# Moving weight splits and time-mix rows to other blocks of a fused FFN stage, and re-ordering the time-mix lists

## The reference, cut to what matters

```python
x = x + 0.5 * L0_ffn(layernorm(x))      # 8 experts, top 2, softmax; shared width 2 x 128
x = x + L0_attn(layernorm(x))           # RWKV: time mix (scan over 256 steps), then channel mix
x = x + 0.5 * L0_ffn(layernorm(x))
x = x + 0.5 * L1_ffn(layernorm(x))      # 8 experts, top 2, sigmoid; shared width 4 x 128
x = x + L1_attn(layernorm(x))           # Mamba-2 with chunks
x = x + 0.5 * L1_ffn(layernorm(x))
```

```python
kvr = norm1(x) @ W_tm;  k, v, r = split(kvr, 3)
k = k * tmk + x_prev * (1 - tmk)        # likewise v; r goes through a sigmoid
y = wkv(time_decay, time_first, k, v)   # recurrence with a running log-sum-exp
x = x + r * y
xn = norm2(x); kk = xn @ W_cm * cmk4 + xp4 * (1 - cmk4)
x = x + sigmoid(xn * cmr + xp * (1 - cmr)) * (square(relu(kk)) @ W_cp)
```

## Time and profile before

| what | value |
|---|---|
| median of 3 runs | 798.79 us (797.66 to 799.57) |
| profiled execution | 803.27 us, of which the span from first to last instruction is 801.5 us |
| mean granted TensorE clock | 0.931 |
| busy share of the span | PE 87%, DVE 71%, ACT 52%, POOL 40% |
| first FFN stage, until PE's first instruction of the next | 142.25 us |
| RWKV stage | 142.25 to 240.3 us |
| all stages behind it | 240.3 to 801.5 us |

### The profile page before, as it was taken

One profiled execution on the slowest core, in us unless ns is written; L12 is line 12 of the kernel. 1 busy time (PEld: TensorE's weight loads), 2 busy tenths in 40 slices (PEclk: granted clock), 3 DMA queues, 4 the chain that ended last, 5 costly groups with the idle time before them and its releaser, 6 DMA issues. The chain is left out here.

```text
span 801.5 us, 12341 instructions
## 1 busy us (share of the span) xinstructions
PE 693.8 (87%) x3996; PEld 511.4 (64%) x3996; DVE 571.6 (71%) x1283; ACT 417.0 (52%) x751; POOL 322.3 (40%) x402
## 2 busy tenths in 40 slices
PE   0979995649887899999999767899999995899997
PEld 0657773324344677777778556677777773677785
DVE  3668796588976888889878675456556665698775
ACT  2535564866523555555555547355555552555553
POOL 1346697210112676545635541322222200356355
PEclk9989997759998999999999967699999997899999
DMA  5244550000000422312122100000000000132222
GB/s 151 87 119 120 151 164 13 0 1 0 2 0 20 140 84 77 105 66 94 59 86 72 49 0 1 1 2 2 1 0 0 0 1 1 68 91 83 77 91 69
DMA packets 32757, 43.10 MB, mean 54 GB/s; under 512 B 5184, under 2 KB 15424, under 8 KB 32704
## 3 DMA queue, kind: packets, MB, share of 16 engines
q1 hardware_dynamic: 32704, 42.46, 17.3%
HBM read 41.13 MB, written 1.31 MB: 53 GB/s over the span
## 5 line engine op out<-in xcount | busy, mean ns | idle before, releaser
L526 POOL TENSOR_TENSOR p_prod<-p_p,p_gate_row 128x512 f32<-128x512 f32 x128 | 201.5, 1583 | 149.6 <-DVE p_p L397 94.5
L303 ACT ACTIVATE p_sil<-p_ps_a 128x512 f32<-128x512 f32 x176 | 105.3, 598 | 142.0 <-PE p_ps_a L100 137.9
L402 DVE TENSOR_TENSOR p_hlo<-p_prod,p_hhi 128x512 fp32r<-128x512 f32 x176 | 152.5, 868 | 0.9 <-ACT p_hhi L312 0.5
L397 DVE TENSOR_TENSOR p_p<-p_sil,p_ps_b 128x512 f32<-128x512 f32 x128 | 87.2, 681 | 64.0 <-ACT p_sil L303 51.1
L312 ACT CAST p_hhi<-p_prod 128x512 fp32r<-128x512 f32 x176 | 108.1, 614 | 31.7 <-POOL p_prod L526 31.4
L98 PE MATMUL p_ps_acc<-p_hhi,w_downhi 128*128 128x512 f32 x176 | 73.0, 415 | 5.2 <-DVE p_hlo L402 5.1
L98 PE MATMUL p_ps_a<-xt_hi,w_uphi 128*128 128x512 f32 x176 | 75.2, 427 | 0.0
L98 PE MATMUL p_ps_b<-xt_hi,w_uphi 128*128 128x512 f32 x176 | 71.7, 407 | 1.6 <-DVE p_p L397 1.2
L99 PE MATMUL p_ps_a<-xt_lo,w_uphi 128*128 128x512 f32 x176 | 70.9, 403 | 0.0
L100 PE MATMUL p_ps_a<-xt_hi,w_uplo 128*128 128x512 f32 x176 | 70.9, 403 | 0.0
L100 PE MATMUL p_ps_b<-xt_hi,w_uplo 128*128 128x512 f32 x176 | 70.6, 401 | 0.0
(11 more groups left out here) (277 smaller groups left out, 1445.2 us busy)
## 6 DMA issues: line engine op xcount, KB each, us to landing
p_gate_row<-gate_rows SPq DMA_DIRECT2D x128, 256.0 KB, 3.3
w_rawbuf<-in_L_ffn_fc_w_dram SPq DMA_DIRECT2D x3, 512.0 KB, 6.3
w_rawbuf<-in_L_ffn_w_dram SPq DMA_DIRECT2D x3, 512.0 KB, 6.0
out_dram<-x SPq DMA_DIRECT2D x4, 256.0 KB, 3.7
w_rawbuf<-in_L_ffn_shared_w_dram SPq DMA_DIRECT2D x3, 256.0 KB, 5.1
mb_xraw<-in_L_attn_W_B_dram SPq DMA_DIRECT2D x1, 512.0 KB, 4.9
mb_xraw<-in_L_attn_W_C_dram SPq DMA_DIRECT2D x1, 512.0 KB, 5.1
gate_rows<-p_gates_t SPq DMA_DIRECT2D x16, 16.0 KB, 1.4
```

The lines of the kernel that those rows point to most:

```text
L303: nc.scalar.activation(sil[:, u % 2], ps_a[:, u % 2], ACT.Silu).then_inc(c["sil"].sem, 1)
L397: nc.vector.tensor_tensor(dst, sil[:, u % 2], ps_b[:, u % 2], ALU.mult).then_inc(c["p1"].sem, 1)
L402: nc.vector.tensor_tensor(hlo[:, u % R], prod[:, u % R], hhi[:, u % R].bitcast(F32), ALU.subtract).then_inc(c["hlo"].sem, 1)
L526: G.tensor_tensor(prod[:, u % R], p1[:, u % 2], gate_row[:, e % ROWS], ALU.mult).then_inc(c["prod"].sem, 1)
```

## The change

The loads change places, the splits go to other slots, three blocks' rows are made in the FFN stage, and the RWKV lists are in another order. `ytok` and `ztok` have four buffers each; `z2tok` and `rg` lose theirs and use the block's `ytok` and `ztok`. The router becomes part 2 of the six weight parts, for both FFNs' weights.

```diff
-    SPLIT_SLOTS = {(2, 5): 0, (2, 6): 1, (2, 7): 2, (3, 0): 3, (3, 3): 4, (3, 5): 5}
+    POOL_SPLITS = {(1, 6): (0,), (1, 7): (1,), (1, 8): (2,), (2, 6): (3,)}
+    DVE_SPLITS = {(BLOCKS - 1, 8): (4, 5)}
+    SPLITS = {**POOL_SPLITS, **DVE_SPLITS}
+    TAIL = BLOCKS - 1
+    NEXT_STATS = {(TAIL - 1, 4): 0, (TAIL - 1, 8): 1, (TAIL, 8): 2}
+    NEXT_SCALES = {(TAIL - 1, 7): 0, (TAIL, 2): 1, (TAIL, 8): 2}
+    NEXT_ROWS = {(TAIL, 1): (0, 0), (TAIL, 2): (0, 1), (TAIL, 5): (1, 0), (TAIL, 6): (1, 1)}
...
@@ ffn_stream, ACT
-                    if splits and (n, p) in SPLIT_SLOTS:
-                        split_hi(nc, act, c, splits[SPLIT_SLOTS[n, p]])
-                    if entry and (n, p) == (BLOCKS - 1, U - 2):
-                        next_tokens(0)
+                    for k in SPLITS.get((n, p), ()) if splits else ():
+                        split_hi(nc, act, c, splits[k])
+                    if entry and (n, p) in NEXT_ROWS:
+                        next_rows(*NEXT_ROWS[n, p])
                 take_out(n)
...
             if entry:
-                next_tokens(1)
+                next_rows(2, 0)
+                next_rows(2, 1)
@@ ffn_stream, DVE: next_stage(n, p), behind gated, low, add_out, choose, normal, low_x, measure
+                if (n, p) in NEXT_STATS:
+                    next_stats(NEXT_STATS[n, p])
+                if (n, p) == (TAIL, 3):
                     prepare_vectors(nc, dve, c, entry["vec"])
+                if (n, p) == (TAIL, 5):
                     prepare_mixing(nc, dve, c, entry["vec"], consts, entry, entry["weights"])
+                    for k in DVE_SPLITS.get((n, p), ()) if splits else ():
+                        split_lo(nc, dve, c, splits[k], k)
...
@@ rwkv_phase, PE
             mix_key(0)
+            mix_key(1)
             mix_val(0)
-            mix_key(1)
...
@@ rwkv_phase, ACT (first entries)
+            take_z(0)
             take_y(0)
-            take_z(0)
+            take_z(1)
             take_y(1)
-            take_z(1)
-            tokens(2)
+            tokens(3)
             decays(0)
-            tokens(3)
             logs(0)
             decays(1)
...
@@ rwkv_phase, DVE
-            measure(2)
             measure(3)
             running_max(0)
...
@@ program
-            jobs.append(((EXPERTS,), [(lambda r: r, router)]) + tuple(t[:] for t in w.router))
+            jobs.insert(2, ((EXPERTS,), [(lambda r: r, router)]) + tuple(t[:] for t in w.router))
...
         def load_rest(sp):
-            w1_set.load(sp, slice(3, None))
-            mb.load(sp)
+            w1_set.load(sp, slice(4, None))
+            rw_set.load(sp)
...
-                           loads=(rw_set.load, lambda sp: w1_set.load(sp, slice(0, 3)), load_rest) if k == 0 else (),
+                           loads=(lambda sp: w1_set.load(sp, slice(0, 4)), load_rest, mb.load) if k == 0 else (),
```

More of the change, by code:

```diff
@@ L565, in body @@
                         scale(n + 3)
[L566 to L569, removed]
+                    for k in POOL_SPLITS.get((n, p), ()) if splits else ():
+                        split_rest(k)
+                    if entry and (n, p) in NEXT_SCALES:
+                        scale_norms(nc, pool, c, consts, entry, NEXT_SCALES[n, p])
             scale(0)
@@ L660, in scale_norms, with apply_norm @@
     G.tensor_tensor(r[:, 5:7], r[:, 2:4], r[:, 4:5].broadcast_to([P, 2, BT]), ALU.mult).then_inc(c["r_rs"].sem, 1)
[L663 to L668, removed]
+def apply_norm(nc, x, entry, m, which):
+    dst, scale, bias = (("ytok", 2, 5), ("ztok", 3, 6))[which]
+    for j in range(BT):
+        r = entry["rs"][:, m]
+        last = nc.scalar.activation(entry[dst][m][:, j], x[:, m * BT + j], ACT.Identity, bias=r[:, bias, j:j + 1],
+                                    scale=r[:, scale, j:j + 1])
     return last
@@ L833, in _ @@
             mix_key(2)
+            grow(2)
             turn_z2(1)
             shrink(0)
+            grow(3)
+            turn_in(3)
             mix_val(2)
-            turn_in(3)
-            grow(2)
+            mix_key(3)
             shrink(1)
-            grow(3)
+            shrink(2)
             mix_rec(2)
-            mix_key(3)
-            shrink(2)
             shrink(3)
@@ L859, in _ @@
             grow(8)
+            grow(9)
             turn_x2(3)
-            grow(9)
+            grow(10)
             shrink(8)
-            grow(10)
             grow(11)
@@ L935, in receive @@
                     act.wait_ge(c["r_p"].sem, c["r_p"].at(m - 1))
-                A(rg[h][:], mixed[4][:], ACT.Tanh, scale=0.5).then_inc(c["r_tr"].sem, 1)
+                A(gate_of(m), mixed[4][:], ACT.Tanh, scale=0.5).then_inc(c["r_tr"].sem, 1)
             def shifted_k(m):
@@ L957, in tokens2 @@
                 for j in range(BT):
-                    last = A(z2tok[h][:, j], key_bank(m)[:, bass.ts(j, P)], ACT.Identity, bias=rs[h][:, 3, j:j + 1],
+                    last = A(ytok[m][:, j], key_bank(m)[:, bass.ts(j, P)], ACT.Identity, bias=rs[h][:, 3, j:j + 1],
                              scale=rs[h][:, 1, j:j + 1])
@@ L1190, in _ @@
             apart(0)
-            lead2(1)
             blend(0)
             output(0)
+            lead2(1)
             received(0)
+            residual(0)
             parts2(1)
-            residual(0)
-            wrap(0)
+            measure2(0)
             numerator(1)
-            measure2(0)
             numerators(1)
@@ L1214, in _ @@
             parts(2)
+            shift(2)
+            square(2)
+            total(2)
+            shift(3)
             gate_in(1)
-            total(2)
-            square(1)
-            shift(2)
             lead2(2)
-            square(2)
+            running_max(3)
             parts2(2)
-            shift(3)
             square(3)
+            lead(3)
             numerator(2)
+            parts(3)
             numerators(2)
-            running_max(3)
-            lead(3)
             gated(0)
-            parts(3)
             apart(2)
+            total(3)
+            blend(2)
             shift(4)
-            blend(2)
-            total(3)
             output(2)
@@ L1255, in _ @@
             received(3)
-            gate_in(2)
             residual(3)
@@ L1263, in _ @@
             square(9)
-            wrap(3)
             shift(10)
+            gate_in(2)
             square(10)
@@ L1268, in _ @@
             square(11)
+            wrap(3)
             gated(2)
-            gate_in(3)
             shift(12)
             square(12)
+            gate_in(3)
             add_out(2)
@@ L2022, in program @@
         for n in ("ytok", "ztok"):
-            entry[n] = [owned(rwkv_scope)(f"rw_{n}{h}", [P, BT, P], F32) for h in range(2)]
+            entry[n] = [owned(rwkv_scope)(f"rw_{n}{h}", [P, BT, P], F32) for h in range(NBLK)]
         entry.update(vec=v, weights=rw)
```

76 lines of the change are left out of this document (39 added, 37 removed).

## The result

The changed kernel takes 788.41 us (median of 4 runs, 786.25 to 791.30), the kernel before 799.18 beside it; the ratio is 0.986, with a 95% interval from 0.982 to 0.991, so 10.8 us less, where 15.8 were forecast. The profiled execution took 788.62 us with a span of 786.9, 14.6 us less than the span of before. That is more than the medians show, since the profiled execution of before (803.27 us) was 4.1 us above the median of the runs beside it. Terms of one or two us are therefore read from the stages in the traces, and the medians only checked against their sum.

A forecast was written before the change was run, and what follows sets the result against it. PE bounds the kernel, busy 87% of the span, losing time where it runs dry or its clock is down; VectorE bounds the later RWKV stage. 5.9 + 0 + 5.4 + 4.5 = 15.8 us, giving 783.0 us; range 777 to 791.

The forecast's parts named there:

- the 18 DMAs: RWKV loads, moved behind row 7 of block 1: block 2's first product 2.3 us late, cost 0, at most 3 us.
- the forecast itself: Outcome of the whole run with a gain of 11 to 18 us, given a chance of 0.57.
- rival 1: Half the gain, 8 us: row 4 late, clock falls, VectorE waits as before; or splits hold VectorE; chance together 0.22.
- The early loads: First FFN's start: row 4 lands 3.1 us earlier, clock stays up for 2.8 more; 5.9 us, bounds 1.4 and 7.1.
- the text's own sign of being wrong: Row 4 still waits for bytes, PE idles in block 1 or 2, or VectorE's idle from the first shift grows.
- the early hole: First FFN: PE dry for 4.85 us since GpSimd waits for row 4 of block 0, with block 1's gates behind.
- The late hole: First FFN's end: earlier last product, sum's copy ahead of row making; 5.4 us, bounds 3.5 and 7.5.
- The RWKV stage: New list order: logs(0) 3.1 us sooner, first shift 3.4, net 1.1 more; 4.5 us, bounds 1.5 and 6.5.
- Rival 2: Whole run: all three parts near their upper bounds, 19.6 us less, 779 us; chance 0.15.
- rival 3: Slower than before: the 18 DMAs delay block 2's rows, first landing at 104 or later; 800 or more, chance 0.04.

The follow-up runs named there:

- e1: Changed kernel with the RWKV stage's three engine lists in the old order (third block's rows stay in the FFN stage); ratio 0.9933 to the kernel before.
- e3: Changed kernel with the 18 RWKV DMAs issued at the FFN stage's start, before the store of block 0's gates; ratio 0.985 to the kernel before.
- e10: Changed kernel with the fourth block's rows, tokens(3), again between decays(0) and logs(0) in ScalarE's RWKV list; ratio 0.990 to the kernel before.
- e2: Changed kernel with VectorE's two splits of the last block moved behind the last add_out; ratio 0.986 to the kernel before.
- e5: Changed kernel measured again without any edit, as the yardstick; 790.00 us, ratio 0.9885 to the kernel before.
- e6: Changed kernel with VectorE's two splits behind the last add_out and GpSimd's fourth split behind its last scales; ratio 0.987 to the kernel before.
- e7: Kernel before with only the load places of the changed one; ratio 0.9967 to the kernel before.
- e4: Changed kernel with weight parts 0 to 3 issued at the FFN stage's start, not between rows 3 and 4 of block 0; ratio 0.983 to the kernel before.
- e8: Changed kernel with weight and RWKV loads at the stage's start, late splits last, third block's statistics and scales earlier, mixing diagonals later; 783.74 us, ratio 0.980.
- e9: e8 with the second block's statistics at position 5 and its scales at position 8 of block 2; 783.47 us, ratio 0.980 to the kernel before.
- e11: e9 with the second block's rows at positions 3 and 4 of the last block and one VectorE split at position 6; 782.76 us, ratio 0.980.

## Why the prediction was right, and where its sizes were off

Each step moved the time in the direction that the text gave, but for the 18 DMAs, and the time lies in the range. The amount was 10.8 us for 15.8, just below the 11 to 18 us that the text calls the forecast itself; the range holds it because it was drawn down to rival 1. The profiled execution, 788.62 us where 787.5 was forecast, comes nearer by luck: 2.5 us of its gain lie in the part that the change does not touch, and 1.2 are the clock.

**The early loads: 3.9 us for 5.9.** The product of row 4 started at 43.5 (44.0 forecast), and PE was dry for 1.99 us (1.7). The term that was mis-sized is the clock: "I take it that it stays up". In this trace it fell: a mean of 0.67 over 5.18 us is 3.4 us at half clock, where before it was 5.58, and gave back 1.1 of the 2.8 us. But behind the same hole of 2.0 us it fell in four traces (after, e1, e3, e10) and stayed up in two (e2, e5), and behind longer ones too (e6, e7); with it up the start is worth 5.3 us (41.86 less 36.55, in e5). The forecast treated as settled what is open from run to run. e4 shows that bytes ahead of the row are 0.6 us of the hole.

**The 18 DMAs in their new place: 0.9 us lost for 0.** Here a step failed, and the text's own sign of being wrong came: PE idled in block 2. The issue took 12.2 us and not 10.4, so that the first product of block 2 came 4.1 us late against PE (85.21, where 85.34 less the 4.2 us of the start was wanted) and not 2.3. That was inside the margin of the text, which let PE stall only from a row about 4 us later still. But it followed only the low parts that PE needs. What PE missed were the gates of block 3, which stand on GpSimd behind those products: its idle time at 96 ends with `p_gates`. It is the same chain that made the early hole. e3 shows that the DMAs' place is the cause.

**The late hole: 3.8 us for 5.4.** Last product, copy ahead of the rows, and then statistics, scales and rows in sequence came as forecast. Mis-sized are the scales of the third block, 4.5 us where 2.8 were taken: VectorE's splits held them, e2 gives back 1.7 us. The text had the rule and its rows at hand, priced it for GpSimd's splits in blocks 1 and 2, where PE had room, and for the stage's end left it in the lower bound.

**The RWKV stage: 5.0 us for 4.5.** `logs(0)` starts 3.1 us sooner against the stage's start, as forecast, and the first `shift` 3.4 us. That the sum fits is partly luck, for the parts are others than in the text: 3.1 us are the order (e1), 0.7 the rows made earlier (e7 to e1, single traces), and 1.2 the clock of these two traces (0.85 and 0.89). Of the 3.1 us at `logs(0)` the order is 2.1 (13.92 in e1, 11.84 now); the text gave all of it to the order. Of the order, one move is 2.4 us (e10). So against the forecast's 4.5 us 3.8 came of the change.

**The rivals.** Rival 1's number (8 us) is nearer to the medians (10.8 and 10.6) than the forecast's 15.8, but of its three causes only one came, the clock that fell: the row was not late, and VectorE does not stand as much as before (6.8 us idle from the first `shift` to the stage's last addition, 7.9 before). GpSimd's splits in blocks 1 and 2 cost nothing: PE is full from 52 to 84, and the fourth one, taken away in e6, moved the last product by 0.3 us. Rival 2 and rival 3 did not come: the first row of block 2 landed at 85, not 104.

What stays open: when the clock falls behind a hole of 2 us; what moves the part behind the RWKV stage between 550.1 and 556.9 us; and why e7's ratio gives 2.6 us where its trace gives 5.2. For the last, the two traces are of a slower and a faster execution than the median (803.27 us, with a median of 800.57 beside e7; 794.57, with 798.78), and the interval just reaches 5.2.

## What to carry to other kernels

Follow a late transfer to everything that stands behind the waiting instruction in its engine's queue, the small instructions above all: here the next block's gates, not the products, were what TensorE missed, twice. Put loads where the issuing queue is empty, even long before they are needed: here 15 us ahead of the first store, where they cost nothing (e3, e4, e8). In a stage's last microseconds keep large VectorE instructions away from small GpSimd ones that something waits for.

## What the runs showed of the hardware

GpSimd instructions of 0.23 and 0.19 us (e2) took 1.11 and 1.03 beside VectorE subtractions of two SBUF inputs of 1024 columns. The other way round, such a subtraction of 1.22 us (e2) took 3.34 beside GpSimd's of 2.34 (e6). In the four traces where the two ran side by side (e6, e8, e9, e11), VectorE's ended 1.08 or 1.09 us behind the end of GpSimd's, whenever it had begun.

The same 18 DMA issues took 8.0 us in a row at the stage's start (e3) and 11.2 in the place behind row 7 of block 1. There, in all eight traces that have it, one issue took 1.87 to 2.37 us and a later one 1.18 to 1.42, where most take 0.43. Weight loads just ahead are not enough to make it: in e8 five of them stand right ahead of the 18, and no issue took over 0.67. What does is not shown.

TensorE's clock stayed up behind holes of 2.00, 2.05, 2.42 and 2.59 us, and fell behind others of 1.99 and 2.00, so the length of this hole alone does not decide it.
